# Attention-image loop of a fused graph kernel: other work of VectorE in every third step, merged ScalarE copies, 26 gather chunks ahead and 13 gathers between segments

## The chip, the cores and the metric

The kernel runs on one core of one Trainium2 chip. The metric is the device time of one execution in microseconds (us). Three runs of the kernel before gave 5274.48, 5282.03 and 5291.11 us, so the median is 5282.03 us.

## The reference

The input is x of shape (32, 64, 48, 48). Cut to what matters here:

```
x  = x + conv(ln_c(x))                 # per image: attention over 2304 pixels
t  = tokens(x);  t = t + ffn(ln_t(t))  # graph attention decides gates, then experts

conv:  xn = xf / max(|xf|, eps)        # 64 channels, P = 2304 pixels
       s  = relu(xn^T xn) ** 2         # P x P
       g  = Wc xf + bc
       out = g s^T
ffn:   h = x W_gat; a_src, a_dst       # 24 numbers for each of 73728 tokens
       262144 random edges + 73728 loops, softmax over the edges into a token
       scores -> top 2 of 4 experts -> 4 gelu MLPs weighted by the gates
```

The edges are sorted inside the kernel, so that the segment softmax becomes a scan along each partition.

## The kernel before

The program has five parts that follow each other on every engine.

1. The first 8 images are computed together with the sorting network of the edges. This part has its own copies of the functions named below and is not touched.
2. The sorted keys are merged and routed.
3. The **image loop** computes the other 24 images (`walk` and `body` from line 1560 on). The first one is written out, then a hardware loop of 8 passes with two images each, a second one of 3 passes with two images each, and the last image written out.
4. The **segment stage** goes over 32 segments of 128 partitions with 82 sorted edges each.
5. The gates and the experts are computed for each image.

*One image of the loop.* 45 steps t. Steps 0 to 35 have a column chunk of 512 pixels (four chunks of 9 steps) and steps 36 to 44 one of 256. In a step TensorE writes `gram` (L1876; eight matmuls, two PSUM banks, two such pairs in alternation). ScalarE writes `rel` from it (relu, L2066). Then in steps with t % 3 == 0 ScalarE squares `rel` into `s2` (L2070), and in the other two VectorE writes `s2` from `gram` and `rel` (L2406). Before the gram of step t, TensorE waits for the reader that frees the bank of step t - 2: VectorE's `s2`, or ScalarE's `rel` where (t - 2) % 3 == 0. After the gram it does `values` of step t - 3 (L1830, `LAG` = 3), which reads `s2`.

Between these steps each engine does other work, at steps that are written out by hand. For the image before: `sums` (residual additions), `post` (16, 16 and 4 matmuls into the PSUM tile `misc`, which ScalarE copies to `c2` and squares into `sq2`), `spread2` and `norm2` (norm of the tokens), `tokens` (transposes). For the image after: `pre` (like `post`, into `cv` and `sq`), `spread`, `scales`, `value_rows`, `units`, `low` on VectorE, `deviation`, `norm`, `high` on ScalarE, and `turn` (transposes) which gives the tile `hl`. The sync engine (SP) swaps the halves of `hl` by two DMAs into `lh`, which the next image's first gram needs. In the 16 images of the first hardware loop, VectorE also does seven `level` calls (four instructions each on 128x328 bytes), at the steps of `LEVEL_AT`.

*Gathers.* GpSimd (POOL) fetches one row of 24 floats from the token table `htab_d` for each of the 262144 edges: 2048 indirect DMAs of 128 rows each (L980), 64 to a chunk (`GC`), with at most 4 in flight. After each chunk the collected `rows` are stored to `raw_d`. The first `AHEAD` chunks (29, so 1856 gathers) are issued while the images run. Then POOL waits for the end of the images (`img_done`), and goes through the segments k = 0 to 31: it issues the loads of segment k (`got` from `raw_d` L1716 and `nb` from `htab_d` L1718, both on POOL's own DMA queue, two buffers), and then `PIECE` (8) further gathers. Ahead of k = 4g the gathers that segments 4g to 4g + 3 need are brought forward where they are missing: 64 x ceil(5.125 (g + 1)) + 10 of them, at most 2048. For k = 20 that is 1994 and for k = 24 it is 2048. Then it waits for the stores of these chunks.

For one segment VectorE runs shifts by predicated copies, two scans over 332 elements and one over 1660. ScalarE lays out the inputs (`AE`, `GT`) and writes the result to `state`, which SP stores to `seg_d`.

Of the kernel before, what the change touches and what calls it, by code (L numbers as in the profile page):

```python
# [18 lines left out]
ALU = mybir.AluOpType  # L19
ACT = mybir.ActivationFunctionType  # L20
# [6 lines left out]
FIRST = 8  # L27
# [1210 lines left out]
def flow(nc, n, Wc, bc, Wg, att_s, att_d, b_gat, gamma, beta, W1, b1, W2, b2):  # L1238
# [7 lines left out]
    PAIRS = QT // 2  # L1246
    STEPS = NCH * PAIRS
    LAG = 3
# [4 lines left out]
    NB = len(BATCH)  # L1253
# [24 lines left out]
    GC, LV = n.GC, n.LV  # L1278
    T = G * W
    CE = CW + 1  # L1280
    AHEAD = 29
    PIECE = 8
    TW = QT
    EW = 384
    ECH = HALF // EW
# [7 lines left out]
    with ExitStack() as ctx, ExitStack() as early, ExitStack() as late:  # L1293
# [197 lines left out]
        r_out = [sem("r_out0"), sem("r_out1")]  # L1491
        block = ctx.enter_context(nc.Block())

        POST_PE = {5 + 2 * i: i for i in range(NB)}
        POST_ACT = {6 + 2 * i: i for i in range(NB)}
        PRE_PE = {19 + 2 * i: i for i in range(NB)}
        PRE_ACT = {20 + 2 * i: i for i in range(NB)}

        def route_of(kind):

# [264 lines left out]
        def _(pe):  # L1765
            n.merge_tensor(pe)
            def pre(b, par, i):

                if i == 0:
                    at_least(pe, n.a_tn, NB * (b - 1))  # L1770
                else:
                    pe.wait_ge(n.a_cv, NB * b + i)
                s0, k = BATCH[i]
                for s in range(s0, s0 + k):
                    for h in range(2):
                        rows = slice(h * C, (h + 1) * C)
                        last = pe.matmul(misc[:, h, (s - s0) * P:(s - s0 + 1) * P], xh[rows, par, s * P:(s + 1) * P], n.wpre[rows, :],
                                         start=True, stop=True)
                last.then_inc(n.pe_pre, 1)

            def turn(b, i):

                q0, k = TBATCH[i]
                if i == 0:
                    pe.wait_ge(n.v_lo, b + 1)
                if i >= 2:
                    pe.wait_ge(n.a_hl, NTB * b + i - 1)
                bank = misc[:, i % 2, :].bitcast(F16)
                for q in range(q0, q0 + k):
                    last = pe.transpose(bank[:, (q - q0) * P:(q - q0 + 1) * P], tw[:, q, :, :].rearrange("p a c -> p (a c)"), n.ident16[:, :])  # L1790
                last.then_inc(n.pe_tr, 1)
# [70 lines left out]
            def body(b, own, par, nth, before, more, moved=None):  # L1862
                pe.wait_ge(n.l_in[par], 32 * (nth + 1))
                for t in range(STEPS):
                    c, k = divmod(t, PAIRS)
                    o, w = CH[c]
                    if t % 3 == 2:
                        pe.wait_ge(a_rel, STEPS * own + (t - 1))
                    else:
                        at_least(pe, v_s2, by_dve(STEPS) * own + by_dve(t - 1))  # L1870
                    bank = gram[(par + t) % 2]
                    for j in (0, 1):
                        for own_words, word in ((True, hl), (False, lh)):
# [9 lines left out]
                    if before and t in POST_PE:  # L1883
                        post(b - 1, 1 - par, POST_PE[t])
                    if before and t == 15:
                        tokens(b - 1, 0)
                        tokens(b - 1, 1)
                    if before and t == 17:
                        tokens(b - 1, 2)
                    if more and t in PRE_PE:  # L1890
                        if t == 19:
                            pe.wait_ge(n.x_in[1 - par], 64 * (nth + 1 + par))
                        pre(b + 1, 1 - par, PRE_PE[t])
                    if more and t == 33:
                        turn(b + 1, 0)
                        turn(b + 1, 1)
                    if more and t == 35:
                        turn(b + 1, 2)
            walk(pe, body)
            for t in range(LAG):  # L1900
# [52 lines left out]
        def _(act):  # L1953
            n.merge_scalar(act)

            def pre(b, i):

                s0, k = BATCH[i]
                act.wait_ge(n.pe_pre, NB * b + i + 1)
                if i == 0:  # L1960
                    at_least(act, n.v_t, b)
                src = misc[:, :, 0:k * P].rearrange("p h (s c) -> p h s c", c=P)
                if k == 4:
                    dst = lambda t: t[:, 0:16, :].rearrange("p (h s) c -> p h s c", h=2)[:, :, s0:s0 + k, :]
                else:
                    dst = lambda t: t[:, 16:18, :].rearrange("p (h s) c -> p h s c", h=2)
                for h in range(2):
                    act.activation(dst(cv)[:, h], src[:, h], ACT.Copy)
                for h in range(2):
                    last = act.activation(dst(sq)[:, h], src[:, h, :, 0:C], ACT.Square)  # L1970
                last.then_inc(n.a_cv, 1)

            def deviation(b):
                act.wait_ge(n.v_ssq, b + 1)
# [16 lines left out]
            def post(b, i):  # L1991
# [6 lines left out]
                for h in range(2):  # L1998
                    act.activation(c2[:, s0:s0 + k, h, :], src[:, h], ACT.Copy)
                for h in range(2):  # L2000
                    last = act.activation(sq2[:, s0:s0 + k, h, :], src[:, h, :, 0:C], ACT.Square)
                last.then_inc(n.a_c2, 1)

            def deviation2(b):
                act.wait_ge(n.v_ssq2, b + 1)
# [52 lines left out]
            def body(b, own, par, nth, before, more, moved=None):  # L2058
                for t in range(STEPS):
# [11 lines left out]
                    if before and t in POST_ACT:  # L2071
                        post(b - 1, POST_ACT[t])
                    if before and t == 12:
                        deviation2(b - 1)
                    if before and t == 16:
                        tokens(b - 1, 0)
                        tokens(b - 1, 1)
                    if before and t == 18:
                        tokens(b - 1, 2)
                    if more and t in PRE_ACT:  # L2080
                        pre(b + 1, PRE_ACT[t])
                    if more and t == 26:
                        deviation(b + 1)
                    if more and t == 28:
                        norm(b + 1)
                    if more and t == 30:
                        high(b + 1)
                    if more and t == 34:
                        turned(b + 1, 1 - par, 0)
                        turned(b + 1, 1 - par, 1)  # L2090
                    if more and t == 36:
                        turned(b + 1, 1 - par, 2)
            walk(act, body)
            for i in range(NB):
# [82 lines left out]
        def _(dve):  # L2177
# [151 lines left out]
            route_step(dve.tensor_copy(slots[0:NR, 0:EC], ext[1][0:NR, 0, :]))  # L2329
            dve.sem_inc(v_xpos, 1)  # L2330

            LEVEL_AT = {9: 0, 15: 1, 18: 2, 24: 3, 33: 4, 36: 5, 42: 6}
            LAST_LEVEL = 44
            LINKED = 4 * LV

# [19 lines left out]
            def starts(g):  # L2355

                dve.tensor_scalar(step_s[:, :], step_d[LV % 2][:, :], 127.5, NEG, ALU.is_gt, ALU.mult).then_inc(vm, 1)
                dve.wait_ge(vm, g * (2 * LINKED + 1) + (LINKED + 1))

            def value_rows(b, par):  # L2360

                dve.tensor_tensor(vr[:, :, :], cv[:, :, C:2 * C], wide(rstd[:, :]), ALU.mult).then_inc(n.pc, 1)
# [23 lines left out]
            def norm2(b):  # L2386
# [8 lines left out]
                dve.tensor_tensor(hx[:, 0:16, :].rearrange("p (h s) c -> p s h c", h=2), c2[:, 0:8, :, C:PW],  # L2395
                                  r[:, 0:8, :].unsqueeze(3).to_broadcast([P, 8, 2, RW]), ALU.mult)
                dve.tensor_tensor(hx[:, 16:18, :], c2[:, 8, :, C:PW], r[:, 8, :].unsqueeze(2).to_broadcast([P, 2, RW]), ALU.mult).then_inc(n.v_t2, 1)
            value_rows(FIRST, 0)

            def body(b, own, par, nth, before, more, moved=None):  # L2400
                for t in range(STEPS):
# [5 lines left out]
                                                 halves(rel[:, t % RELS, 0:2 * w]), ALU.mult, ALU.mult).then_inc(v_s2, 1)  # L2407
                    if before and t == LAG:
                        sums(b - 1, 1 - par, nth - 1 + par, NCH - 1)
                    if t % PAIRS == LAG and t > PAIRS:  # L2410
                        sums(b, par, nth, t // PAIRS - 1)
                    if before and t == 11:
                        spread2(b - 1)
                    if before and t == 13:
                        norm2(b - 1)
                    if more and t == 25:
                        spread(b + 1)
                    if more and t == 27:
                        scales(b + 1)
                    if more and t == 28:  # L2420
                        value_rows(b + 1, 1 - par)
                    if more and t == 29:
                        units(b + 1)
                    if more and t == 31:
                        low(b + 1)
                    if moved and t in LEVEL_AT:
                        level(moved[0], moved[1], LEVEL_AT[t])
                    if moved and t == LAST_LEVEL:
# [254 lines left out]
```

## Time and profile before

| what | us |
|---|---|
| median of three runs | 5282.03 |
| the profiled execution, its own time | 5291.28 |
| its span in the profile | 5289.5 |
| TensorE busy in the span | 3533.1 (67%) |
| VectorE busy | 3964.2 (75%) |
| ScalarE busy | 3392.4 (64%) |
| GpSimd busy | 2941.6 (56%) |

The span is the time from the first to the last record. The profile has a busy share for each engine, the waits with what ended them, the instructions in order of time, and groups of them by source line. A time such as 3658.60 is counted in us from the start of the span. Durations of neighbouring instructions of one engine overlap by about 0.1 us, so that a distance between two starts is the better measure of what an instruction takes. The image loop lies from 1409 to 3650, the segment stage from there to about 4272.

### The profile page before, as it was taken

The numbers are of one execution on the slowest core, as the hardware profiler recorded it, in microseconds if no ns is written. First come the engines' busy times: TensorE is split into PE (matmuls) and PEld (weight loads), VectorE is DVE, ScalarE is ACT, GpSimd is POOL, SyncE is SP. The second block draws the span as 40 slices with busy tenths as digits, with TensorE's granted clock in tenths as the row PEclk, the third lists the DMA queues.
The fourth block names the chain that finished last, engine by engine and source line by source line (L and its number), as shares of the span: only waits on it lengthen the run. The fifth ranks groups of instructions, "written<-read, shape, count | busy, mean of one in ns | idle before, by whom it ended". The sixth has DMA issues, their size and how long they took to land. (4 is left out here: it accounts for less than half of the span.)

```text
span 5289.5 us, 70597 instructions
## 1 busy us (share of the span) xinstructions
PE 3533.1 (67%) x22687; PEld 1450.6 (27%) x22687; DVE 3964.2 (75%) x5512; ACT 3392.4 (64%) x4285; POOL 2941.6 (56%) x2937
## 2 busy tenths in 40 slices
PE   4888988500488888888898988884000017788778
PEld 1223333200243344343443444342000002222222
DVE  8998988997666666766666655555999848787877
ACT  4777988401676767776676776775566526566665
POOL 6000000048777777777777777777656147666661
PEclk9999999755699999999999999997555558888889
DMA  6100100002122222222222212224555527999997
GB/s 258 36 20 20 33 21 16 17 14 82 22 47 57 42 62 48 47 52 52 56 48 46 64 40 53 48 50 105 176 190 187 190 71 147 151 161 159 155 157 141
DMA packets 332482, 441.96 MB, mean 84 GB/s; under 512 B 183193, under 2 KB 261916, under 8 KB 331500
## 3 DMA queue, kind: packets, MB, share of 16 engines
q1 hardware_dynamic: 209744, 288.12, 19.8%
q0 software_dynamic: 105536, 148.61, 16.6%
q8 instruction: 187, 3.06, 0.2%
q10 hardware_dynamic: 16896, 1.18, 0.2%
q14 instruction: 119, 0.97, 0.1%
HBM read 252.35 MB, written 166.47 MB: 79 GB/s over the span
## 5 line engine op out<-in xcount | busy, mean ns | idle before, releaser
L980 POOL DMA_INDIRECT rows<-htab_d,idx x2048 | 2134.3, 1042 | 761.3 <-issue 603.9
L2406 DVE SCALAR_TENSOR_TENSOR s<-gram,rel 128x1024 f32<-128x1024 f32 (+1 forms) x720 | 798.1, 1116 | 800.1 <-ACT rel L2066 797.3
L2066 ACT ACTIVATE rel<-gram 128x1024 f32<-128x1024 f32 (+1 forms) x1080 | 1005.4, 940 | 540.5 <-PE gram L1876 533.1
L1830 PE MATMUL acc<-s,gT 128*64 128x512 f32 (+1 forms) x4320 | 1020.2, 552 | 0.0
L1876 PE MATMUL gram<-hl 128*64 128x512 f16 (+1 forms) x4320 | 787.9, 367 | 217.5 <-DVE s L2406 182.3
L1876 PE MATMUL gram<-hl,lh 128*64 128x512 f16 (+1 forms) x4320 | 775.5, 361 | 13.5 <-issue 13.5
L1761 POOL DMA_INDIRECT R<-seg_d,nidx x576 | 587.7, 1020 | 191.3 <-issue 165.9
L1930 PE MATMUL ye<-hid,w 128*64 128x384 f32 x1536 | 376.2, 570 | 260.5 <-DVE ms L2625 195.8
L1080 POOL IOTA slots<- 64x2048 int32 x1 | 1.8, 1833 | 975.5 <-POOLq L192 975.5
L2158 ACT ACTIVATE hid<-up,b1t 128x768 f32<-128x768 f32 x384 | 333.8, 900 | 261.4 <-PE up L1942 260.1
L1876 PEld LDWEIGHTS gram<-hl 128*64 128x64 f16 x4320 | 244.5, 110 | 708.2 <-DVE s L2406 467.3
L1913 PE MATMUL tailsT<-ident,tails 128*20 128x128 f32 x24 | 5.2, 412 | 610.6 <-DVE tails L2513 610.6
L906 ACT ACTIVATE w_s2r<-w_gram 128x1024 f32<-128x1024 f32 (+1 forms) x360 | 349.4, 971 | 94.0 <-PE w_gram L775 93.5
L316 DVE TENSOR_TENSOR edges<-edges 128x2048 f32<-128x2048 f32 (+1 forms) x186 | 370.8, 1994 | 47.7 <-ACT edges L935 42.1
L1942 PE MATMUL up<-tne,w 64*128 64x384 f32 x1536 | 397.7, 599 | 3.1 <-DMA x2e<-x_d 2.5
L317 DVE TENSOR_TENSOR edges<-edges 128x2048 f32<-128x2048 f32 (+1 forms) x186 | 369.7, 1987 | 0.0
L888 ACT ACTIVATE w_s2r<-w_s2r 128x1024 f32<-128x1024 f32 (+1 forms) x360 | 362.1, 1006 | 0.0
L749 PE MATMUL w_acc<-w_s2r,w_gT 128*64 128x512 f32 (+1 forms) x1440 | 361.2, 581 | 1.1 <-ACT w_s2r L888 1.1
L2070 ACT ACTIVATE s<-rel 128x1024 f32<-128x1024 f32 (+1 forms) x360 | 349.8, 972 | 11.5
L2625 DVE SCALAR_TENSOR_TENSOR ms<-ye,b2c,gs 128x384 f32<-128x384 f32 x384 | 232.0, 616 | 152.2 <-PE up L1942 92.3
L1830 PEld LDWEIGHTS acc<-s,gT 128*64 128x64 f32 x4320 | 298.8, 138 | 155.8 <-issue 3.3
L1876 PEld LDWEIGHTS gram<-hl,lh 128*64 128x64 f16 x4320 | 246.3, 111 | 236.9 <-issue 134.5
(372 smaller groups left out, 5401.4 us busy)
## 6 DMA issues: line engine op xcount, KB each, us to landing
gs<-gates_d SPq DMA_DIRECT2D x64, 1024.0 KB
rows<-htab_d,idx POOLq DMA_INDIRECT x2048
seg_d<-state SPq DMA_DIRECT2D x32, 996.0 KB, 8.9
raw_d<-w_zeros POOLq DMA_DIRECT2D x48, 512.0 KB, 23.2
raw_d<-rows POOLq DMA_DIRECT2D x32, 768.0 KB
tne<-tn_d SPq DMA_DIRECT2D x32, 576.0 KB
x2e<-x_d SPq DMA_DIRECT2D x32, 576.0 KB
out<-res SPq DMA_DIRECT2D x64, 256.0 KB
```

The source lines that it names most:

```text
L316: dve.tensor_tensor(lo, a, b, ALU.min)
L317: step(dve.tensor_tensor(hi, a, b, ALU.max))
L749: last = pe.matmul(acc[(b + c) % 2][j * C:(j + 1) * C, 0:w], gT[:, b % 2, 2 * k + j, :], s2(s)[:, j * w:(j + 1) * w], start=k == 0, stop=k ...
L888: act.activation(s2(s)[:, 0:2 * w], rel(s)[:, 0:2 * w], ACT.Square).then_inc(a_s2, 1)
L980: pool.indirect_dma_start(out=n.rows[:, k % 2, j, :], out_offset=None, in_=n.htabx, in_offset=bass.IndirectOffsetOnAxis(ap=n.idx[:, g % 2, ...
L1761: pool.indirect_dma_start(out=R[:, par, j, :], out_offset=None, in_=n.seg, in_offset=bass.IndirectOffsetOnAxis(ap=nidx[:, par, j:j + 1], a ...
L1830: last = pe.matmul(acc[(par + c) % 2][j * C:(j + 1) * C, 0:w], gT[:, par, 2 * k + j, :], s2[:, u % SLOTS, j * w:(j + 1) * w], start=k == 0 ...
L1876: last = pe.matmul(bank[h * C:(h + 1) * C, j, 0:w], word[:, par, first_pixel:first_pixel + C], hl[:, par, o:o + w], start=own_words, stop= ...
L1930: last = pe.matmul(y[i % 2][h * C:(h + 1) * C, 0:EW], w2[:, k, :], hid[:, i % GROUP, h, :], start=True, stop=True)
L1942: last = pe.matmul(up[i % GROUP][:, h, 0:EW], w1[rows_, k, :], tne[rows_, par, cp * EW:(cp + 1) * EW], start=True, stop=True)
L2066: act.activation(rel[:, t % RELS, 0:2 * w].rearrange("p (j x) -> p j x", j=2), gram[(par + t) % 2][:, :, 0:w], ACT.Relu, scale=1.0 / SPLIT ...
L2406: dve.scalar_tensor_tensor(halves(s2[:, t % SLOTS, 0:2 * w]), gram[(par + t) % 2][:, :, 0:w], 1.0 / SPLIT ** 2, halves(rel[:, t % RELS, 0: ...
```

## The change

The image loop gets another timetable. `post` is done by TensorE and ScalarE in the same steps 5, 8, 11, `pre` in 14, 17, 20 (before: TensorE 5, 7, 9 and 19, 21, 23, ScalarE one step later). All other work of VectorE moves to steps with t % 3 == 0, in which it has no `s2` to write. `value_rows` is cut in two, its second half goes to step 0 of the next image. ScalarE's two copies and two squares of each batch become one copy and one square over both PSUM banks. POOL gathers 26 chunks ahead instead of 29, and 13 gathers follow each segment's loads instead of 8.

```diff
-    AHEAD = 29
-    PIECE = 8
+    AHEAD = 26
+    PIECE = 13
...
-        POST_PE = {5 + 2 * i: i for i in range(NB)}
-        POST_ACT = {6 + 2 * i: i for i in range(NB)}
-        PRE_PE = {19 + 2 * i: i for i in range(NB)}
-        PRE_ACT = {20 + 2 * i: i for i in range(NB)}
+        POST_AT = {5 + 3 * i: i for i in range(NB)}
+        PRE_AT = {14 + 3 * i: i for i in range(NB)}
...  TensorE
-                    if before and t == 15:
+                    if before and t == 23:
+                        if more:
+                            pe.wait_ge(n.a_cv, NB * (b + 2))
                         tokens(b - 1, 0)
                         tokens(b - 1, 1)
-                    if before and t == 17:
+                    if before and t == 26:
                         tokens(b - 1, 2)
-                    if more and t == 33:
+                    if more and t == 35:
                         turn(b + 1, 0)
                         turn(b + 1, 1)
-                    if more and t == 35:
+                    if more and t == 36:
                         turn(b + 1, 2)
...  ScalarE, in pre; post alike with c2 and sq2
-                for h in range(2):
-                    act.activation(dst(cv)[:, h], src[:, h], ACT.Copy)
-                for h in range(2):
-                    last = act.activation(dst(sq)[:, h], src[:, h, :, 0:C], ACT.Square)
-                last.then_inc(n.a_cv, 1)
+                act.activation(dst(cv), src, ACT.Copy)
+                act.activation(dst(sq), src[:, :, :, 0:C], ACT.Square).then_inc(n.a_cv, 1)
...  ScalarE's steps: deviation2 12 -> 17, tokens 16, 18 -> 23, 26, deviation 26 -> 25,
...  norm 28, high 30 -> 32, turned 34, 36 -> 35, 37
...  VectorE
-            LEVEL_AT = {9: 0, 15: 1, 18: 2, 24: 3, 33: 4, 36: 5, 42: 6}
+            LEVEL_AT = {6: 0, 9: 1, 12: 2, 15: 3, 21: 4, 27: 5, 42: 6}
+            SUMS_AT = {12: 0, 21: 1, 33: 2, 39: 3}
+            def value_scaled(b):
+                dve.tensor_tensor(vr[:, :, :], cv[:, :, C:2 * C], wide(rstd[:, :]), ALU.mult).then_inc(n.pc, 1)
...
-                    if t % PAIRS == LAG and t > PAIRS:
-                        sums(b, par, nth, t // PAIRS - 1)
-                    if before and t == 11:
+                    if before and t == 0:
+                        value_rows(b, par)
+                    if more and t == 33:
+                        low(b + 1)
+                    if t in SUMS_AT:
+                        sums(b, par, nth, SUMS_AT[t])
+                    if before and t == 15:
                         spread2(b - 1)
-                    if before and t == 13:
+                    if before and t == 18:
                         norm2(b - 1)
-                    if more and t == 25:
+                    if more and t == 24:
                         spread(b + 1)
                     if more and t == 27:
                         scales(b + 1)
-                    if more and t == 28:
-                        value_rows(b + 1, 1 - par)
-                    if more and t == 29:
+                    if more and t == 30:
                         units(b + 1)
-                    if more and t == 31:
-                        low(b + 1)
+                    if more and t == 36:
+                        value_scaled(b + 1)
```

## Rows read from the trace of the kernel before

**Rows 1.** By stretch: length, busy PE, PEld, DVE, ACT, POOL, PEclk, DMA share, GB/s
```profile
1409.00:2519.00 1110.00, 971.84 (x7515) 440.54 (x7511) 727.56 (x988) 785.21 (x1100) 837.28 (x842) 0.98 0.23 49
...
3881.00:3955.00 74.00, 0.00 (x0) 0.00 (x0) 68.52 (x115) 44.60 (x33) 43.37 (x41) 0.50 0.56 183
...
4111.00:4270.00 159.00, 1.13 (x6) 0.79 (x7) 142.72 (x236) 91.91 (x67) 22.03 (x17) 0.50 0.47 159
```

**Rows 2.** SP in order of time: start, us, operation (first DMA of a swap, `img_done`)
```profile
1489.03 0.46 SPq L1580 DMA_DIRECT2D lh<-hl  x1
...
3540.36 0.50 SPq L1580 DMA_DIRECT2D lh<-hl  x1
...
3650.15 0.38 SPq L1634 DMA_DIRECT2D pos<-xpos_d  x1
```

**Rows 3.** Groups of instructions: count, busy us, mean ns, idle before and its releasers
```profile
L1876 PE MATMUL gram<-hl 128*64 128x512 f16 (+1 forms) x4320 | 787.9, 367 | 217.5 <-DVE s L2406 182.3
...
L1804 PE MATMUL misc<-wpost,x 64*128 64x88 f32 x858 | 65.3, 286 | 24.8 <-ACT sq L2001 23.5 <-DVE x L2379 1.3
...
L2066 ACT ACTIVATE rel<-gram 128x1024 f32<-128x1024 f32 x864 | 880.1, 1026 | 469.4 <-PE gram L1876 462.0 <-DVEq L2330 3.8 <-issue 1.9
...
L1968 ACT ACTIVATE cv<-misc 128x512 f32<-128x512 f32 x92 | 49.7, 598 | 0.0
...
L2379 DVE TENSOR_TENSOR x<-acc,half 64x512 f32<-64x512 f32 x96 | 66.6, 694 | 3.3
...
L2351 DVE SCALAR_TENSOR_TENSOR step_t<-step_m,step_d 128x328 uint8<-128x328 uint8 x96 | 48.5, 505 | 3.3
```

**Rows 4.** TensorE in order of time, one image and the restart ahead of it
```profile
2434.45 0.64 PE L1876 MATMUL gram<-hl 128*64 128x512 f16 x2 [2.66 <-issue]
...
2459.36 0.41 PE L1876 MATMUL gram<-hl 128*64 128x512 f16 x2
...
2464.85 0.38 PE L1876 MATMUL gram<-hl 128*64 128x512 f16 x2
...
2466.57 0.38 PE L1876 MATMUL gram<-hl 128*64 128x512 f16 x2
...
2478.71 1.02 PE L1830 MATMUL acc<-s,gT 128*64 128x512 f32 x4
...
2480.76 0.41 PE L1876 MATMUL gram<-hl 128*64 128x512 f16 x2
```

**Rows 5.** All engines in order of time, one step from gram to s2
```profile
2634.65 0.38 PE L1876 MATMUL gram<-hl 128*64 128x512 f16 x2
...
2635.80 1.02 ACT L2066 ACTIVATE rel<-gram 128x1024 f32<-128x1024 f32 x1 [0.42 <-PE gram L1876]
...
2636.86 1.23 DVE L2406 SCALAR_TENSOR_TENSOR s<-gram,rel 128x1024 f32<-128x1024 f32 x1 [0.22 <-ACT rel L2066]
```

**Rows 6.** POOL in order of time, segment stage, idle before and releaser in brackets
```profile
3658.60 0.95 POOL L1716 DMA_INDIRECT got<-raw_d,edge  x1 [0.30 <-issue]
...
3674.95 1.14 POOL L1716 DMA_INDIRECT got<-raw_d,edge  x1 [0.30 <-DMA rows<-htab_d,idx]
...
3899.96 1.11 POOL L1716 DMA_INDIRECT got<-raw_d,edge  x1 [0.30 <-issue]
...
3912.34 1.40 POOL L980 DMA_INDIRECT rows<-htab_d,idx  x1 [4.68 <-DMA rows<-htab_d,idx]
...
3917.96 0.95 POOL L1716 DMA_INDIRECT got<-raw_d,edge  x1 [0.30 <-issue]
...
4102.01 0.95 POOL L980 DMA_INDIRECT rows<-htab_d,idx  x1 [0.30 <-issue]
...
4111.06 0.96 POOL L1716 DMA_INDIRECT got<-raw_d,edge  x1 [5.55 <-issue]
```

**Rows 7.** The chain that ended last, in order of time: start, us, what
```profile
4112.33 7.57 DMA nb<-htab_d,node
...
4268.32 3.52 ACT state L2123
```

**Rows 8.** Line L980 alone, from 1410 to 3410: its gathers
```profile
L980 POOL DMA_INDIRECT rows<-htab_d,idx x1498: 942/947/3015, 1409.6 to 3409.7; - x188
```

More of the change, by code:

```diff
@@ L1769, in pre @@
                 if i == 0:
-                    at_least(pe, n.a_tn, NB * (b - 1))
+                    at_least(pe, n.a_c2, NB * (b - 1))
                 else:
@@ L1785, in turn @@
                     pe.wait_ge(n.v_lo, b + 1)
+                    at_least(pe, n.a_tn, NB * (b - 1))
                 if i >= 2:
@@ L1882, in body @@
                         values(b - 1, own - 1, 1 - par, STEPS + t - LAG)
-                    if before and t in POST_PE:
-                        post(b - 1, 1 - par, POST_PE[t])
-                    if before and t == 15:
+                    if before and t in POST_AT:
+                        post(b - 1, 1 - par, POST_AT[t])
+                    if more and t in PRE_AT:
+                        if PRE_AT[t] == 0:
+                            pe.wait_ge(n.x_in[1 - par], 64 * (nth + 1 + par))
+                        pre(b + 1, 1 - par, PRE_AT[t])
+                    if before and t == 23:
+                        if more:
+                            pe.wait_ge(n.a_cv, NB * (b + 2))
                         tokens(b - 1, 0)
                         tokens(b - 1, 1)
-                    if before and t == 17:
+                    if before and t == 26:
                         tokens(b - 1, 2)
[L1890 to L1893, printed above, removed]
-                    if more and t == 33:
+                    if more and t == 35:
                         turn(b + 1, 0)
                         turn(b + 1, 1)
-                    if more and t == 35:
+                    if more and t == 36:
                         turn(b + 1, 2)
@@ L1961, in pre @@
                     at_least(act, n.v_t, b)
+                    at_least(act, n.v_g, b)
                 src = misc[:, :, 0:k * P].rearrange("p h (s c) -> p h s c", c=P)
@@ L1997, in post @@
                 src = misc[:, :, 0:k * PW].rearrange("p h (s c) -> p h s c", c=PW)
[L1998 to L2002, printed above, removed]
+                by_half = lambda t: t[:, s0:s0 + k, :, :].rearrange("p s h c -> p h s c")
+                act.activation(by_half(c2), src, ACT.Copy)
+                act.activation(by_half(sq2), src[:, :, :, 0:C], ACT.Square).then_inc(n.a_c2, 1)
             def deviation2(b):
@@ L2070, in body @@
                         act.activation(s2[:, t % SLOTS, 0:2 * w], rel[:, t % RELS, 0:2 * w], ACT.Square).then_inc(a_s2, 1)
-                    if before and t in POST_ACT:
-                        post(b - 1, POST_ACT[t])
-                    if before and t == 12:
+                    if before and t in POST_AT:
+                        post(b - 1, POST_AT[t])
+                    if more and t in PRE_AT:
+                        pre(b + 1, PRE_AT[t])
+                    if before and t == 17:
                         deviation2(b - 1)
-                    if before and t == 16:
+                    if before and t == 23:
                         tokens(b - 1, 0)
                         tokens(b - 1, 1)
-                    if before and t == 18:
+                    if before and t == 26:
                         tokens(b - 1, 2)
-                    if more and t in PRE_ACT:
-                        pre(b + 1, PRE_ACT[t])
-                    if more and t == 26:
+                    if more and t == 25:
                         deviation(b + 1)
@@ L2085, in body @@
                         norm(b + 1)
-                    if more and t == 30:
+                    if more and t == 32:
                         high(b + 1)
-                    if more and t == 34:
+                    if more and t == 35:
                         turned(b + 1, 1 - par, 0)
                         turned(b + 1, 1 - par, 1)
-                    if more and t == 36:
+                    if more and t == 37:
                         turned(b + 1, 1 - par, 2)
@@ L2358, in starts @@
                 dve.wait_ge(vm, g * (2 * LINKED + 1) + (LINKED + 1))
+            def value_scaled(b):
+                dve.tensor_tensor(vr[:, :, :], cv[:, :, C:2 * C], wide(rstd[:, :]), ALU.mult).then_inc(n.pc, 1)
             def value_rows(b, par):
-                dve.tensor_tensor(vr[:, :, :], cv[:, :, C:2 * C], wide(rstd[:, :]), ALU.mult).then_inc(n.pc, 1)
                 dve.wait_ge(n.pc, b + 2)
@@ L2397, in norm2 @@
                 dve.tensor_tensor(hx[:, 16:18, :], c2[:, 8, :, C:PW], r[:, 8, :].unsqueeze(2).to_broadcast([P, 2, RW]), ALU.mult).then_inc(n.v_t2, 1)
+            value_scaled(FIRST)
             value_rows(FIRST, 0)
```

## The prediction

> **What bounds the kernel now.** I read the busy time by stretch first, to cut the span into stages. In the image loop TensorE is the fullest engine: 971.84 us of 1110, at the full clock (granted 0.98, so 2.4 GHz nearly throughout) [rows 1]. In the segment stage TensorE does nothing; VectorE is busy 68.52 us of 74, which is four segments, so 18.5 us a segment. After the last gather it goes on at the same pace [rows 1]. So a faster image loop and a slower segment stage are the two things to weigh.
>
> Next, the waits. Between the first DMAs of two swaps lie one or more images: (3540.36 - 1489.03) / 22 = 93.24 us for an image [rows 2]. Of TensorE's idle time before grams, 182.3 us end with VectorE's `s`, and 23.5 us before `post` end with ScalarE's square [rows 3]. TensorE is late because the timetable puts VectorE's other work between a `rel` and the `s` that frees a bank.
>
> Last, POOL. It never stops gathering in the image loop. Images end at 3650.15 [rows 2], yet the first `got` leaves at 3658.60 [rows 6]: POOL is 8.4 us late. In the segment stage one turn of POOL takes 3917.96 - 3899.96 = 18.0 us, with 4.68 us in which it waits for its own rows behind `got` and `nb` [rows 6]. It has no slack against VectorE's 18.5 us. The image loop and POOL end together, and in the segments VectorE and POOL are equally slow. A change that shifts gathers from the one stage to the other is paid in full.
>
> **The image loop after.** *TensorE's own work.* A full step costs 2466.57 - 2464.85 = 1.72 us [rows 4]; I take half of it for the nine narrow steps: 36 x 1.72 + 9 x 0.86 = 69.7 us. A batch of 16 small matmuls adds: from `values` to the next gram 2480.76 - 2478.71 = 2.05 us with `pre` between them, 0.86 without, so 1.19 us [rows 4]. I count seven and a half of these in an image (`post`, `pre`, `tokens`, `turn`, the small third batches at a third to a half): 8.9 us. Sum 78.6 us. The change moves this work and removes none.
>
> *What the bank chain adds.* Gram start to `rel` start is 1.15 us, to `s` start 2.21, and with the 1.23 us of `s` 3.44 [rows 5]: just two steps of TensorE. After a step t % 3 == 0 ScalarE has `rel` and the square (2.1 us) before the next `rel`, which makes that one some 0.3 us late. Three full steps therefore take 5.49 us (2464.85 - 2459.36) and not 5.16 [rows 4]. With 1.19 us of other matmuls in step 3n + 2 the chain has cover: TensorE then sets the pace with 6.35 us for the three. So what is left over TensorE's own 78.6 us is: about 0.3 us in each of five groups of three with little or no such work, 1.6 in steps 0 to 2 (their `values` are narrow, the chain isn't), 0.6 in each of three narrow groups; together 5.0 us. The restart of the hardware loop stays: once in two images, 2.66 us of idle time end with "issue", and the grams behind it take 0.64 us at the half clock (1.2 GHz) instead of 0.38 [rows 4]; with a second such gap of 1.8 us and a dozen slow matmul groups I estimate 5.4 us, 2.7 for an image. After: 78.6 + 5.0 + 2.7 = 86.3 us. Gain 93.24 - 86.3 = 6.9 us, over 22.5 images (first and last have half of the other work) **156 us**.
>
> *Why the moved work costs nothing there.* VectorE's gap between the `s` of a step 3n + 2 and that of 3n + 4 is about 2.5 us, and 3.6 where TensorE has a batch in between. The largest pairs are a level (four instructions of at most 0.505 us: 2.0) with sums (two of 0.694: 1.4), so 3.4 us [rows 3], in steps 12 and 21; the `s` behind them is 0.3 to 0.5 us late and the batch in steps 14 and 23 covers it. Without that cover it would be 0.5 us x 2 x 16 = 16 us. *Merged copies.* 1024 elements take 1.026 us and 512 take 0.598, so a merged copy saves 2 x 0.598 - 1.026 = 0.17 us [rows 3]; with the square some 0.35 us a batch, 2 us an image on ScalarE. It isn't the bound; the saving only keeps the next `rel` from being late, and is in the 5.0 us. If a copy over two banks cost more than two copies, 0.4 us in six places would come back: 2.4 us an image. *Waits.* `tokens` waits for `pre`'s copies (step 20, three steps earlier), with the next gram behind it in TensorE's queue; `pre` on ScalarE waits for `value_rows` of step 0: both long past. `turned` of the third batch comes one step later, and SP's swap with it. Now the swap has from 1489.03 to the next image's gram some 8.8 us and lands in time; it will have 7.5. That is at most 1.3 us an image, 0 to 30 us. I take 0, since 576 KB are small against the 2 MB that land within 9 us below.
>
> Bounds of the gain: 90 us (half of the stalls come back in other places) to 190 us (only the loop restart and the narrow steps' 3.4 us are left).
>
> **The segment stage after.** By 3410 the kernel before has issued 166 + 1498 = 1664 gathers, 166 of them ahead of 1410 [rows 8]: that is AHEAD = 26 exactly. Images end at 3650.2 - 156 = 3494, so POOL stands idle for 84 us, and the 8.4 us of lateness go. 384 gathers instead of 192 are left.
>
> *One turn of POOL.* `got`, `nb`, 4 gathers, the wait until both have landed, then 9 gathers instead of 4. A gather that waits for nothing is 1.25 us. The first turn before, when no `state` is being stored, takes 3674.95 - 3658.60 = 16.35 us [rows 6]: with five more 22.6. A later one, with a store beside it, takes up to 18.5, the pace of the whole stage [rows 1]: with five more 24.8. Lower end: `nb` of k = 24 has landed 8.8 us after `got` left (4112.33 + 7.57 - 4111.06) [rows 6, 7]; the fourth gather's wait then ends at 10.1 and the turn at 21.35. With POOL behind VectorE the store of `state` falls some 11 us after a `got` leaves, so `got` no longer shares the DMA engines with it; I take **23.0**, nearest to the first turn.
>
> *The sum.* 24 turns x 23.0 = 552. At k = 20, 1664 + 20 x 13 = 1924 of 1994 gathers are there: 70 at one stretch, 70 x 1.25 = 87.5 us. Such a barrier ends with a store, 4111.06 - 4102.01 - 0.95 = 8.1 us [rows 6]; it is passed at k = 20 and, with two gathers, at k = 24: 18.7. From `got` of k = 24 to the end 4268.32 - 4111.06 = 157.3 [rows 6, 7]. Together 552 + 87.5 + 18.7 + 157.3 = 815 us, against 4268.3 - 3658.6 = 609.7 before: **205 us longer**. The end moves from 4268.3 to 3494 + 815 = 4309: +41 us. What follows is untouched.
>
> The Trainium skill, page "DMA: Bandwidth & Descriptors", section "Queues, rings and completion order", says that an engine takes the descriptors of one ring in order and takes turns between the rings of several queues. The wait of 4.68 us agrees with the first half. By the second half a `got` that no longer runs beside a store would land earlier, which speaks for the lower end, 21.35, and is rival 1.
>
> Against the profiled execution: 5291.3 + 41 = 5332. That one is 9 us above the median of the runs, 5282, so the forecast for the median is **5323 us**, slower by 0.8%.
>
> **The rivals.**
> 1. *Short turns.* The loads land undisturbed, 21.35 us a turn: 24 x 1.65 = 40 us less, so 5283. With the gain at its upper end of 190 us it is 5249. From 21.3 us a turn, at my 156 us, the change isn't slower. For it: the landing in [rows 7]. Against it: with a store or the chunk store beside it, the turn was 18.0 and not 15.1 [rows 6].
> 2. *Issue alone.* If the wait behind `got` and `nb` went away, 15 instructions x 1.25 = 18.75 us, close to VectorE's 18.5: 24 x 4.25 = 102 us less, 5221. Against it: the wait has its place in nearly every turn, and only 4 gathers can be in flight.
> 3. *The timetable stalls elsewhere.* The gain is 100 us or less, because ScalarE's evacuation in step 3n + 2 delays both following `rel`, or because the swap lands late: 5379. For it: ScalarE's square already holds up `post` for 23.5 us [rows 3]. Against it: ScalarE has 785.21 us of work in 1110 [rows 1], and loses 2 us an image of it.
>
> **Chances.** About 0.3% (16 us) is what can be told from no change. Forecast 0.48 (slower 0.42, same 0.06), rival 1 0.22 (same 0.12, faster 0.10), rival 2 0.12 (faster), rival 3 0.14 (slower), mixtures 0.04 (same). Faster 0.22, same 0.22, slower 0.56. The range 5245 to 5385 leaves rival 2 out; the forecast's own range is 5285 to 5370.
>
> **What would show it.** Right: images 86 to 87 us apart in the swaps; idle before grams for VectorE's `s` down to some 60 us; `got` of k = 0 right behind `img_done` near 3494, POOL idle ahead of it; distances of 22 to 24 us between `got`s, with VectorE waiting for `AE` or ScalarE for `nb`; a stretch of 70 gathers ahead of k = 20. Wrong: turns of about 18.5 us, a last gather before 4102, or images over 89 us apart.

## The result and the profile after

The changed kernel is slower: 5343.56 us, the median of four runs (5338.44 to 5347.99), against 5282.90 for the kernel before on the same chip (four runs, 5274.48 to 5291.11). The ratio is 1.0115, 95% interval 1.0096 to 1.0133. The profiled execution took 5342.47 us, with a span of 5340.6 us.

The end of the images first. SP in order of time: two swaps with an image of the level loop between them that holds no loop restart, the next swap after one that does, and `img_done`.

```profile
2457.75 0.53 SPq L1578 DMA_DIRECT2D lh<-hl  x1
...
2540.36 0.51 SPq L1578 DMA_DIRECT2D lh<-hl  x1
...
2638.97 0.53 SPq L1578 DMA_DIRECT2D lh<-hl  x1
...
3504.32 0.38 SPq L1632 DMA_DIRECT2D pos<-xpos_d  x1
```

The images end at 3504.32 instead of 3650.15 [rows 2]: 146 us gained. A plain image takes 82.6 us; before, the same distance was 91.0. But the image with the restart takes 94.6 to 98.6 us in all seven places of the level loop, where before it took 96.4 to 98.3. Almost the whole gain of those images is eaten by something new, which the waits of VectorE name (columns: who waits for whom, us in total, times, longest; 1409 to 3490):

```profile
DVE s L2406 <- ACT rel L2063: 555.3, 478, 8.4
...
DVE step_m L2348 <- SPq L1623: 49.0, 6, 10.4
...
DVE step_m L2348 <- issue: 6.0, 1, 6.0
```

In the kernel before (1409 to 3650, line 1625 there) VectorE waited at this point once:

```profile
DVE step_m L2350 <- SPq L1625: 2.3, 1, 2.3
```

Line 1623 is the point at which SP has seen the stores of `step_m` and `step_s` land and lets VectorE write `step_m` again (`moves_free`). In order of time, SP issues the stores and VectorE gets on, first in one pass and then, in a second fence, in another with TensorE behind it:

```profile
2565.82 2.71 SPq L1621 DMA_DIRECT2D start_d<-step_s  x1
...
2576.04 0.33 DVE L2348 TENSOR_SCALAR step_m<-shift 128x328 uint8 x1 [10.44 <-SPq L1623]
```

```profile
1681.87 0.33 DVE L2348 TENSOR_SCALAR step_m<-shift 128x328 uint8 x1 [7.17 <-SPq L1623]
...
1683.97 2.36 DVE L2406 SCALAR_TENSOR_TENSOR s<-gram,rel 128x1024 f32<-128x1024 f32 x2
...
1685.25 0.64 PE L1875 MATMUL gram<-hl 128*64 128x512 f16 x2 [4.70 <-DVE s L2406]
```

The `s` stands in VectorE's queue behind the waiting level, and TensorE behind the `s`: 4.70 us idle, and its first grams after it take 0.64 us where others take 0.38. The granted clock is 0.50 from 1685 to 1688 (1.2 GHz) and 1.00 from 1692 to 1700 (2.4 GHz).

By stretch (length, then busy PE, PEld, DVE, ACT, POOL with counts, PEclk, DMA share, GB/s), and two groups of the page's list:

```profile
1409.00:2519.00 1110.00, 1030.73 (x8003) 481.90 (x7999) 777.07 (x1056) 833.61 (x1026) 837.23 (x851) 0.96 0.24 51
...
3520.00:3945.00 425.00, 0.00 (x0) 0.00 (x0) 321.29 (x537) 206.92 (x149) 336.31 (x279) 0.50 0.47 155
```

```profile
PE 3516.5 (66%) x22687; PEld 1467.8 (27%) x22687; DVE 3973.7 (74%) x5512; ACT 3389.7 (63%) x3997; POOL 2965.9 (56%) x2937
...
L1875 PE MATMUL gram<-hl 128*64 128x512 f16 (+1 forms) x4320 | 801.4, 368 | 135.3 <-DVE s L2406 95.1
```

In the same 1110 us TensorE now issues 8003 matmuls instead of 7515 [rows 1], and its idle time for `s` is 95.1 us instead of 182.3 [rows 3]. In the segment stage VectorE is busy 321 us of 425: 76%, where it was 93% [rows 1]. It has become the one that waits.

POOL in order of time: the `got` of k = 0, 19, 20 and 24; and the last `state` in the chain of waits.

```profile
3504.52 0.94 POOL L1714 DMA_INDIRECT got<-raw_d,edge  x1 [112.36 <-SPq L1631]
...
3945.61 0.95 POOL L1714 DMA_INDIRECT got<-raw_d,edge  x1 [0.30 <-issue]
...
4063.15 0.96 POOL L1714 DMA_INDIRECT got<-raw_d,edge  x1 [3.25 <-DMA raw_d<-rows]
...
4162.74 0.96 POOL L1714 DMA_INDIRECT got<-raw_d,edge  x1 [3.73 <-issue]
```

```profile
4320.27 3.53 ACT state L2120
```

A turn takes (3945.61 - 3504.52) / 19 = 23.2 us. From k = 19 to k = 20 it is 117.5 us, and from `got` of k = 24 to the end 157.5. The stage is 815.8 us long, against 609.7. The sum: 206 us lost, 146 + 8 (POOL no longer late) gained, so 52 us later at the last `state`; the rest of the kernel is as long as before, and the profiled executions differ by 51 us.

The inside of a turn (POOL and VectorE) is where the time goes:

```profile
3689.34 0.95 POOL L980 DMA_INDIRECT rows<-htab_d,idx  x1 [0.30 <-issue]
...
3690.42 1.53 DVE L2504 TENSOR_TENSOR G<-GT,G 128x1312 f32<-128x1312 f32 x1 [0.55 <-ACT G L2113]
3690.59 2.18 POOL L1714 DMA_INDIRECT got<-raw_d,edge  x1 [0.30 <-issue]
...
3691.98 3.62 DVE L2507 TENSOR_TENSOR_SCAN S<-G 128x1660 f32<-128x1660 f32 x1
...
3693.07 3.28 POOL L1716 DMA_INDIRECT nb<-htab_d,node  x1 [0.30 <-issue]
...
3696.66 0.95 POOL L980 DMA_INDIRECT rows<-htab_d,idx  x1 [0.30 <-issue]
```

`got` takes 2.18 and `nb` 3.28 us to issue where they take 0.95 alone: `got` begins inside the multiply `G` and ends 0.82 us after it (at 3691.95), `nb` begins inside the scan `S` and ends 0.75 us after it (at 3695.60). Every turn has one issue of each kind. In 3520 to 3945 eighteen issues begin inside a multiply and end 0.81 or 0.82 us behind its end (5 `got`, 6 `nb`, 7 gathers, 1.86 us on average), and eighteen begin inside a scan and end 0.75 us behind its end (2 `got`, 5 `nb`, 11 gathers, 3.28 us). POOL's groups in 3520 to 3945 (count, busy us, mean ns, idle before) show it for all turns, and those of the burst ahead of k = 20, 3970 to 4058, in which VectorE is busy for 4 us of 88, show the issue without it:

```profile
L980 POOL DMA_INDIRECT rows<-htab_d,idx x239 | 273.7, 1145 | 78.0 <-issue 70.1 <-DMA rows<-htab_d,idx 7.9
L1716 POOL DMA_INDIRECT nb<-htab_d,node x18 | 33.7, 1874 | 5.5 <-issue 5.5
...
L1714 POOL DMA_INDIRECT got<-raw_d,edge x18 | 27.3, 1518 | 5.5 <-issue 5.5
```

```profile
L980 POOL DMA_INDIRECT rows<-htab_d,idx x68 | 67.6, 995 | 20.7 <-issue 20.1 <-DMA rows<-htab_d,idx 0.6
```

So in 18 turns POOL waits 7.9 us for rows, 0.4 us in each, where the prediction's 23.0 us hold 23.0 - 18.75 = 4.25 us of waiting. The turn is 15 x 1.25 = 18.75 us of issue, 0.4 of waiting, and some 4 us in which issues are held up: 3.28 - 0.95 = 2.3 us by the scan, 1.86 - 0.95 = 0.9 us by the multiply, and some 0.8 in small pieces beside VectorE's shorter instructions.

### The profile page after: what moved, and what is told of

The parts are those of the page before. It is cut to its first block and busy times, and to the rows that moved or that the text cites. A ratio compares the mean times of both kernels' runs of the same rounds, so it can differ in the third digit from the quotient of the medians.

```text
span 5340.6 us, 70355 instructions
## 1 busy us (share of the span) xinstructions
PE 3516.5 (66%) x22687; PEld 1467.8 (27%) x22687; DVE 3973.7 (74%) x5512; ACT 3389.7 (63%) x3997; POOL 2965.9 (56%) x2937
## 5 line engine op out<-in xcount | busy, mean ns | idle before, releaser
L980 POOL DMA_INDIRECT rows<-htab_d,idx x2048 | 2131.2, 1041 | 671.1 <-issue 599.6
L1829 PE MATMUL acc<-s,gT 128*64 128x512 f32 (+1 forms) x4320 | 1035.7, 556 | 0.9 <-issue 0.9
L1875 PE MATMUL gram<-hl 128*64 128x512 f16 (+1 forms) x4320 | 801.4, 368 | 135.3 <-DVE s L2406 95.1
L1875 PE MATMUL gram<-hl,lh 128*64 128x512 f16 (+1 forms) x4320 | 790.5, 364 | 0.0
## 6 DMA issues: line engine op xcount, KB each, us to landing
raw_d<-w_zeros POOLq DMA_DIRECT2D x48, 512.0 KB, 23.2
```

The costliest lines, as they stand in the source:

```text
L980: pool.indirect_dma_start(out=n.rows[:, k % 2, j, :], out_offset=None, in_=n.htabx, in_offset=bass.IndirectOffsetOnAxis(ap=n.idx[:, g % 2, ...
L1829: last = pe.matmul(acc[(par + c) % 2][j * C:(j + 1) * C, 0:w], gT[:, par, 2 * k + j, :], s2[:, u % SLOTS, j * w:(j + 1) * w], start=k == 0 ...
```

## Experiments

The runs were made on several chips, each with the kernel before beside it, so ratios to it are compared, and places in the trace.

**The timetable alone.**

```diff
-    AHEAD = 26
-    PIECE = 13
+    AHEAD = 29
+    PIECE = 8
```

> The changed kernel with AHEAD = 29 and PIECE = 8 as before, so the timetable and the merged copies alone. Theory (image loop and POOL end together, a shorter image loop is worth nothing while 1856 gathers must be out first): images end near 3504 as in the changed kernel, but the first got leaves at about 3392 + 192 x 1.27 = 3636 to 3645, and 610 us of segments follow: the end moves from 4268 to about 4250, total 5273 us, 0.3% faster than before. Rival (the image loop's 146 us arrive whole): 5145 us.

Measured: 5298.44 against 5313.14 us, ratio 0.9964 (0.9950 to 0.9979). The images end at 3510.84, the first `got` leaves at 3647.60, a turn takes 18.5 us, the last `state` is at 4254.0. With 29 chunks ahead POOL is still gathering until 3647: the first `got` leaves 11 us earlier than before and the last `state` comes 14 us earlier, of the 139 us that the images gain. The size was the expected one.

**The gathers alone.** The kernel before, with only the two numbers changed (the edit is shown against the kernel before).

```diff
-    AHEAD = 29
-    PIECE = 8
+    AHEAD = 26
+    PIECE = 13
```

> The kernel before with AHEAD = 26 and PIECE = 13, nothing else. Theory: got of k = 0 at 3650, turns of 23.2 us, 117 us at k = 20, 815 us of segments: the end moves from 4268 to 4466, total 5488 us, 3.7% slower than before. Rival (the wait behind got and nb gives way when there are more gathers, turns of 18.75 us by issue alone): 5385 us.

Measured: 5513.79 us, ratio 1.0372 (1.0351 to 1.0392). First `got` at 3646.85, turns of (4085.56 - 3646.85) / 19 = 23.1 us, last `state` at 4461.2. The price of the moved gathers is that of the prediction, about 200 us, and doesn't depend on the timetable.

**The first level no longer at step 6.**

```diff
-            LEVEL_AT = {6: 0, 9: 1, 12: 2, 15: 3, 21: 4, 27: 5, 42: 6}
+            LEVEL_AT = {9: 0, 12: 1, 15: 2, 21: 3, 24: 4, 27: 5, 42: 6}
```

> The changed kernel with LEVEL_AT = {9, 12, 15, 21, 24, 27, 42} instead of {6, 9, 12, 15, 21, 27, 42}: the first level waits for SP's store of the last group's moves, and comes three steps later. Theory (the wait of 7 us at step 6 stalls TensorE by 4.7 us and its clock falls behind it, some 7.7 us in each of 7 to 8 passes): image loop 55 to 62 us shorter, got of k = 0 near 3446, segments unchanged at 815 us, total 5283 us, 1.1% faster than the changed kernel. Rival (the long interval at steps 8 and 9 is the restart of the hardware loop moved to another place): no change from 5343 us.

Measured: 5323.84 us, ratio 1.0022 (1.0012 to 1.0031), so 0.93% or 49 us under the changed kernel; in the trace the last `state` comes 43 us earlier (4277.1). The waits of VectorE and TensorE and the end of the images in it:

```profile
DVE step_m L2348 <- SPq L1623: 13.9, 5, 4.1
```

```profile
PE gram L1875 <- DVE s L2406: 62.0, 126, 2.4
```

```profile
3462.68 0.38 SPq L1632 DMA_DIRECT2D pos<-xpos_d  x1
```

The restart images fall to 87.7 to 91.8 us, the plain ones stay at 82.6. TensorE's idle time for `s` is 62.0 us, and the images end 42 us earlier, where 55 to 62 were expected. The restart itself did not move: the rival is out. 14 us of the wait remain at step 9.

**Eight gathers in flight.** (Four semaphores are shared for it.)

```diff
-IN_FLIGHT = 4
+IN_FLIGHT = 8
```

> The changed kernel with up to 8 gathers in flight instead of 4 (four other semaphores are shared to make room). Theory (4 in flight make POOL wait behind got and nb; with 8 it issues through the 10 us that they need): turns of 19 to 20 us instead of 23.2, 24 x 3.7 = 90 us less, total about 5255 us. Rival (the DMA engines or POOL's queue set the turn, and more gathers in flight only wait there): turns stay near 23 us, total 5343 us.

Measured: 5371.29 us, ratio 1.0112 (1.0095 to 1.0129): no change from 1.0115. The turn is (3942.74 - 3509.57) / 19 = 22.8 us. POOL's waits for rows are gone, and the issues behind `got` are as long as ever (waits 3400 to 4200, then POOL in order of time):

```profile
POOL rows L980 <- DMA rows<-htab_d,idx: 2.4, 8, 0.3
```

```profile
3689.31 2.18 POOL L1712 DMA_INDIRECT nb<-htab_d,node  x1 [0.30 <-issue]
...
3691.80 3.29 POOL L980 DMA_INDIRECT rows<-htab_d,idx  x1 [0.30 <-issue]
```

The theory that the landing behind `got` and `nb` sets the turn is out.

**A shorter last scan.**

```diff
-  dve.tensor_tensor_scan(S[:, :, :, :] ..., G0[:, :, :, :] ..., G1[:, :, :, :] ..., 0.0, ALU.mult, ALU.add)
+  dve.tensor_tensor_scan(S[:, 0, :, :] ..., G0[:, 0, :, :] ..., G1[:, 0, :, :] ..., 0.0, ALU.mult, ALU.add)
```

> The changed kernel with the last scan of each segment over the first head alone (415 elements instead of 1660; the sums of the other three heads are left out and stay zero). Theory A (POOL's indirect DMAs take 2.7 us instead of 0.95 while VectorE scans, and that makes the turn 23.2 us and not 18.75 plus a short wait): turns fall by 2 to 2.5 us to about 21, total 50 to 60 us below the changed kernel, 1.001 of before. Theory B (the turn is 15 issues and the wait for got and nb): VectorE's shorter segment changes nothing, turns stay at 23.2 us and the total 1.1% above before, less 15 to 20 us at the end of the stage where VectorE sets the pace.

Measured: 5286.14 us, ratio 0.9998 (0.9986 to 1.0010). The turn is (3910.97 - 3505.93) / 19 = 21.3 us, 1.9 shorter. POOL's groups, 3520 to 3945:

```profile
L980 POOL DMA_INDIRECT rows<-htab_d,idx x262 | 268.2, 1024 | 97.8 <-issue 73.2 <-DMA rows<-htab_d,idx 24.7
L1716 POOL DMA_INDIRECT nb<-htab_d,node x19 | 24.9, 1311 | 5.8 <-issue 5.8
L1714 POOL DMA_INDIRECT got<-raw_d,edge x19 | 19.9, 1049 | 5.8 <-issue 5.8
```

Issues are shorter in all three groups, and the wait for rows comes back: 24.7 us in 19 turns. No issue begins inside the shortened scan any more. But in each of the 19 turns one begins inside the multiply and ends 0.80 to 0.83 us behind its end, 1.77 us on average, as with the full scan (1.86): the multiply holds it up by itself. Not all of the total is the turn's: from `got` of k = 24 to the last `state` it is 138.4 us instead of 157.5, 19 us less, since the scan is on VectorE's path there.

**Short scan and eight in flight together.** Both edits above.

> The changed kernel with both the short last scan (it goes over the first head only; the sums of the other three heads are left out and stay zero) and 8 gathers in flight instead of 4 (four semaphores are shared for it). Each alone has run: the short scan brought a turn of POOL from 23.2 to 21.3 us and brought back waits of 1.1 to 2.0 us behind `got` and `nb`; 8 in flight alone left the turn at 22.8. Theory (the two lie beside each other: the issue is held up by the scan for 3.5 us behind `got`, and that same time hides the landing): with both gone a turn is 15 issues x 1.25 = 18.75 plus what is still held up by the multiply and the last quarter of the scan, 1.2 to 1.5 us, so 20.0 to 20.3 us, with no wait for rows; about 19 x 1.2 = 23 us and a few more under the short scan alone, ratio to before about 0.995. Rival (the waits behind `got` and `nb` aren't a matter of the number in flight, the queue itself is full): the turn stays at 21.3, ratio 1.000.

Measured: 5266.28 us, ratio 0.9956 (0.9942 to 0.9970). Turn (3895.99 - 3506.65) / 19 = 20.5 us. Its waits of POOL, 3520 to 3900:

```profile
POOL rows L980 <- DMA rows<-htab_d,idx: 0.9, 3, 0.3
```

That is 0.8 us a turn under the short scan alone, in which no waits for rows are left; with the full scan the same eight in flight gave 0.4. So the two costs lie in part beside each other: while the scan holds up the issues, the loads land. Taken away one at a time they bring 0.4 and 1.9 us, together 2.7, and 1.7 remain over bare issue. The turn is a little over the expected 20.0 to 20.3 us.

**Split copies.** The late level, with two copies and two squares for each batch again.

```diff
-                act.activation(dst(cv), src, ACT.Copy)
-                act.activation(dst(sq), src[:, :, :, 0:C], ACT.Square).then_inc(n.a_cv, 1)
+                for h in range(2):
+                    act.activation(dst(cv)[:, h], src[:, h], ACT.Copy)
...
```

> The changed kernel with LEVEL_AT from 9 on, and ScalarE's copies and squares for each half as before the change: the timetable without the merged copies. Theory (with a batch every third step ScalarE has slack; its 2 us an image are not on the path): images 82.6 to 83 us apart, as in the run with the levels from step 9 on, total within 0.2% of it (1.0022 of before). Rival (the merged copies carry a good part of the image loop's gain): 2 to 3 us an image, 50 us or 1% slower than that run.

Measured: 5306.66 us, ratio 1.0029 (1.0015 to 1.0043), beside 1.0022 with merged copies. Plain images take 82.8 us in the level loop and 83.0 behind it, against 82.6. The merging is worth 0.2 to 0.4 us an image.

**VectorE's other work one step later,** in steps t % 3 == 1, on top of the late level.

```diff
-            LEVEL_AT = {9: 0, 12: 1, 15: 2, 21: 3, 24: 4, 27: 5, 42: 6}
-            SUMS_AT = {12: 0, 21: 1, 33: 2, 39: 3}
+            LEVEL_AT = {10: 0, 13: 1, 16: 2, 22: 3, 25: 4, 28: 5, 43: 6}
+            SUMS_AT = {13: 0, 22: 1, 34: 2, 40: 3}
...  all others of VectorE one step later too
```

> The changed kernel with the levels from step 9 on, and then all of VectorE's other work (levels, sums, norms) one step later, so in steps t % 3 == 1, in which VectorE also writes s2. Everything else as it is. Theory (the gain of the image loop is that VectorE has its other work where it has no s2 to write): each piece delays the s2 behind it by its whole length less the little idle time, images 88 to 91 us apart instead of 82.6, and the end of the images near 3600 instead of 3460. Rival (the gain comes from the batches of post and pre every third step): images stay within 1 us of 82.6.

Measured: 5649.52 us, ratio 1.0685 (1.0643 to 1.0728). TensorE's wait, and the end of the images:

```profile
PE gram L1875 <- DVE s L2406: 299.4, 270, 2.7
```

```profile
3798.86 0.38 SPq L1632 DMA_DIRECT2D pos<-xpos_d  x1
```

Plain images take 99.5 to 100.3 us in the level loop and 92.6 to 93.9 without levels, against 82.6. The direction is the expected one, the size more than twice that: 17 us an image, not 6 to 8. The run does not move VectorE's work alone in its effect, since ScalarE and TensorE kept their steps for what hangs on it: TensorE now waits 41.4 us in the 23 `turn`s for VectorE's `tw`, and ScalarE 58.7 us for `ssq` and 48.7 for `n`, where the late level has no such waits of note. So the run shows that the place of VectorE's work matters much; how much of the 17 us is the `s2` behind it, it does not separate.

**Batches every second step** (matmuls at 5, 7, 9 and 14, 16, 18, ScalarE a step later), on top of the late level.

```diff
-        POST_AT = {5 + 3 * i: i for i in range(NB)}
-        PRE_AT = {14 + 3 * i: i for i in range(NB)}
+        POST_AT = {5 + 2 * i: i for i in range(NB)}
+        PRE_AT = {14 + 2 * i: i for i in range(NB)}
+        POST_ACT = {6 + 2 * i: i for i in range(NB)}
+        PRE_ACT = {15 + 2 * i: i for i in range(NB)}
```

> The changed kernel with the levels from step 9 on, and post in TensorE's steps 5, 7, 9 and pre in 14, 16, 18, ScalarE's part one step behind each, as before the change; VectorE's timetable stays. Theory (ScalarE has 1.38 us of a step's own work and 1.4 to 1.6 of a merged batch, so with a batch every second step it needs 2.1 to 2.2 us a step where TensorE needs 1.72 and half a batch, 2.3): about even, images 0 to 2 us longer than 82.6. Rival (the pace of a third step for batches is most of the gain): 4 to 6 us longer.

Measured: 5352.70 us, ratio 1.0124 (1.0091 to 1.0157). Images 85.1 us apart instead of 82.6. The 2.5 us lie between what theory and rival expected; the every-third-step place of the batches has a share of its own in the gain. Of the 91.0 - 82.6 = 8.4 us of a plain image these 2.5 and the 0.2 of the copies leave 5.7 us for VectorE's timetable and the rest, if the shares add up. That is a remainder and not a measurement: no run has the old steps of VectorE with all else new, and `pre` lay in 19, 21, 23 before and not in 14, 16, 18.

**A version that beats both.** Late level one place later still, 27 chunks ahead, 11 gathers a segment.

```diff
-    AHEAD = 26
-    PIECE = 13
+    AHEAD = 27
+    PIECE = 11
...
-            LEVEL_AT = {6: 0, 9: 1, 12: 2, 15: 3, 21: 4, 27: 5, 42: 6}
+            LEVEL_AT = {12: 0, 15: 1, 21: 2, 24: 3, 27: 4, 30: 5, 42: 6}
```

> The changed kernel with LEVEL_AT = {12, 15, 21, 24, 27, 30, 42}, AHEAD = 27 and PIECE = 11. Theory: the wait for the store of the moves is gone (17 us were left of it at step 9), images end near 3446, 1728 gathers are out near 3473, which is then the start; turns of 24 x 19.9 us, 66 and 21 us at k = 20 and 24, 157 us to the end: 4194, total 5217 on the chip of the first profile, 1.4% faster than the kernel before. Rival (any split of the gathers ends at the same time, since POOL is the limit throughout): about 0.3% faster, as with 29 and 8.

Measured: 5251.97 us, ratio 0.9936 (0.9917 to 0.9954), about half of what was hoped for. The images end at 3467.05, the first `got` leaves 25 us later, at 3492.23, with POOL still gathering until then; turns take 20.3 us. No wait for `moves_free` is left, but the plain images of the level loop take 83.4 us. In it a level shares step 30 with `units`; whether that is the cause was not tried.

## Why the prediction came out as it did

**The forecast held**: slower, 5343.6 in 5245 to 5385, and 20 us above the forecast value. Of these, 10 are the images' end (3504 and not 3494). The other 10 are the step from the profiled execution to the median: I took 9 us off, as the kernel before has them; after, the profiled execution lies 1 us under the median.

*The image period.* Without a restart the forecast was 78.6 + 5.0 = 83.6 us, measured 82.6. TensorE's idle time for `s` was forecast at "some 60" us: 95.1 in the changed kernel, 62.0 with the level later. The sum of own work and bank chain was 1.0 us too dear; which of its terms was, no run separates. That VectorE's place matters is shown by the run one step later, +17 us an image, though not all of it by way of `s2`.

*"Why the moved work costs nothing there": the step that failed.* I listed the waits of `tokens`, `pre`, `turned` and the swap, and left out the one behind the first `level`: moving it from step 9 to step 6 puts it ahead of SP's release of `step_m`, whose stores are issued behind the loads and stores of that image. The restart images take 96.0 us on average with it and 89.7 with the level later: 6.3 us a pass, and 43 to 49 us of the total. The 156 us came out nearly right (146) because errors of opposite sign met, which was luck: in seven places the restart image costs 96.0 - 82.6 = 13.4 us and not 5.4, 56 us too little in the forecast, while plain images are 1.0 us better than forecast and a restart outside the level loop costs 2.2 us or less. Without most of the wait the gain is 3650.2 - 3462.7 = 187 us, close to the upper bound of 190, and even then the kernel isn't faster than before (1.0022).

*The restart*, forecast 5.4 us once in two images: 5.4 to 7.3 before (96.4 to 98.3 beside 91.0), and 5 to 9 with the late level, part of which is the wait that remains. In the second loop, where VectorE has no levels, it is only 2.1 and 2.2 us in the changed kernel (84.7 and 84.8 beside 82.6), and 5.5 to 7.2 us in the level loop of the version with no such wait (88.9 to 90.6 beside 83.4): the restart costs more where there are levels, and no run shows why. *The swap* in time: the plain images show no loss. *Merged copies* off the path: right.

*POOL's idle time*: 84 forecast, 112.4 measured; 10 of it are the images' end, the rest is POOL, which ended its 1664 gathers earlier than before. Right in kind, and free.

*The turn*: 23.0 forecast, 23.2 measured, **for another reason than the one written**. I built it from a wait until `got` and `nb` have landed, and 1.25 us for every gather. The wait is 0.4 us a turn. In its place whatever POOL issues beside VectorE's scan or multiply is held up, some 4 us a turn, and the loads land meanwhile. Rival 2, that the wait goes away and the turn falls to 18.75, had its condition met and not its price.

The lower end of 21.35 is what the short scan alone gave (21.3): but at most 1.3 us (24.7 / 19) of its 2.6 over bare issue is the wait, the rest is slow issue, so that agreement too is one of sums.

The agreement of 23.0 with 23.2 was luck. The kernel before had both costs: in its turns of 3700 to 4030 the multiply meets no issue, since POOL is waiting for its rows then, and one gather begins in each scan, late enough to lose 2.48 - 0.95 = 1.5 us on average (the 1.40 us at 3912.34 in [rows 6] is one of these). In the stretch 3700 to 3955 the wait is 4.0 us a turn (55.3 in all) and slow issue 2.1. With five more gathers a turn, issues begin in the multiply too and earlier in the scan: the wait falls to 0.4 us and slow issue grows to 4.

*The burst, the barriers, the tail*: 118.6 forecast and 117.5 measured from k = 19 to 20; 157.3 and 157.5 for the tail; 815 and 815.8 for the stage.

Rival 1 (short turns) and rival 3 (stalls elsewhere, 100 us of gain or less) did not come; rival 3's kind did, in a place that it hadn't named.

What stays open: of the 1.7 us a turn over bare issue that are left with the short scan and eight in flight, 0.9 are the issue that begins in the multiply (1.82 us on average, 18 times), and the rest is spread over issues of up to 1.5 us beside VectorE's shorter instructions, which no run tells apart. Open too is how the 17 us an image of the work one step later divide.

## What to carry to other kernels

Work that is shifted from a stage with cover to one without is paid in full; price it first, at the receiving stage's own rate. When an instruction is moved to an earlier step, list every semaphore that it waits for and what releases each, DMA completions above all, since everything behind it in its queue waits too. And where a sum agrees with a measurement, look whether its terms do.

## What the runs showed of the hardware

An indirect DMA of 128 rows takes POOL 0.95 us to issue when VectorE is idle (mean 0.995 in 68), and 3.28 us when its issue begins 1.1 us into a VectorE scan with two inputs of 1660 elements (3.62 us). An issue that begins inside the scan ends 0.75 us behind its end, in all 18 cases after and in all 18 of 3700 to 4040 before, where one that begins 0.24 us into the scan takes 4.13 us. One that begins inside the multiply with two inputs of 1312 elements (1.53 us) ends 0.81 us behind its end, in all 18. But one that is already 0.48 us old when the multiply begins still takes 0.95 us (10 of 10): what is under way by then is not held up. With the scan cut to a quarter, `nb` falls from 1.87 to 1.31 us and `got` from 1.52 to 1.05. The Trainium skill, "GPSIMD Engine Reference", in its key points, says that GpSimd shares its SBUF interfaces with VectorE and contends with VectorE instructions that have two SBUF inputs; this trace agrees. The Trainium skill, "SBUF — State Buffer", section "Who interferes with whom", says that `tensor_tensor` with two SBUF inputs contends with GpSimd's reads, but that a probe did not show it stalling a DMA, and names no scan; here a multiply with two inputs, and a scan, both hold up the issues of indirect DMAs. For the scan the run that shortens it shows this. For the multiply the rows show it: no run takes it out, but the issues that begin in it keep their length (1.86 and 1.77 us) when the scan behind it is cut to a quarter.
